# AdaLN attention and expert layer: a new order of work ahead of the first attention step

## The reference

```python
mod = (silu(c) @ wmod).reshape(1, 6, 1, 256)       # sa, ca, ga, sb, cb, gb
h = layernorm(x) * (1 + ca) + sa
q = (h @ Wq).reshape(1024, 16, 16); k = (h @ Wk).reshape(1024, 4, 16); v = (h @ Wv).reshape(1024, 4, 16)
q, k = rope(q), rope(k)                            # rotates the first 8 of the 16 numbers of a head
attn = softmax(q @ k.T * 16 ** -0.5)               # 4 query heads share a head of k and v
x = x + ga * (attn @ v) @ Wo
```

## Time and profile before

| what | us |
|---|---|
| median of 3 runs (528.10, 524.89, 522.38) | 524.89 |
| profiled execution, its own time | 527.01 |
| its span, first to last instruction | 525.2 |
| TensorE, VectorE, ScalarE, GpSimd busy | 467.3, 344.1, 217.1, 208.3 |
| mean granted clock of TensorE | 0.947 |

### The profile page before, as it was taken

How to read it: one execution, slowest core, us unless ns; L and a number is a source line. 1 busy time by engine, 2 the same in 40 slices (tenths; PEclk the granted TensorE clock), 3 DMA queues, 4 the chain that set the end, 5 groups by cost and what they waited for, 6 DMA issues and landing times.

```text
span 525.2 us, 7847 instructions
## 1 busy us (share of the span) xinstructions
PE 467.3 (89%) x2748; PEld 250.5 (48%) x2748; DVE 344.1 (66%) x751; ACT 217.1 (41%) x317; POOL 208.3 (40%) x209
## 2 busy tenths in 40 slices
PE   3958889999999999997896999899999998999890
PEld 3635222333333333223664767566666666666560
DVE  5597959999999999902276973655545454455247
ACT  1547437878878788794213231111111111111140
POOL 3366000212032021200312244567777777776503
PEclk9987769999999999999597999999999999999996
DMA  8970000000000000000101001068888888884181
GB/s 282 337 216 0 1 0 2 1 1 1 1 2 1 1 2 2 0 1 1 40 0 41 1 1 29 13 198 256 271 258 252 244 265 244 278 262 146 38 338 61
DMA packets 33617, 53.68 MB, mean 102 GB/s; under 512 B 6870, under 2 KB 21918, under 8 KB 33584
## 3 DMA queue, kind: packets, MB, share of 16 engines
q1 hardware_dynamic: 27728, 44.82, 26.8%
q0 software_dynamic: 5856, 8.43, 5.6%
HBM read 50.71 MB, written 10.09 MB: 116 GB/s over the span
## 4 chain that ended last, share of the span: by engine, by line
PE 58%; DVE 18%; DMA 9%; issue 6%; POOL 5%; ACT 4%; SPq 0%; DVEq 0%; POOLq 0%; ACTq 0%
PE PV L1221 12%; DMA ychoice<-QS,tab 8%; PE M L1175 7%; PE EP L1403 7%; PE EP L1208 5%; PE EP L1211 5%; PE EP L1299 4%; DVE mx L788 2%; POOL QS L449 2%; PE PV L1420 2%; DVE x L1056 2%; POOL ychoice L454 2%; PE M L1420 1%; DMA x<-in_x 1%; DVE QS L1008 1%
## 5 line engine op out<-in xcount | busy, mean ns | idle before, releaser
L788 DVE TENSOR_REDUCE mx<-M 128x1 f32<-128x512 f32 x256 | 159.3, 683 | 18.0 <-PE M L1175 17.8
L607 ACT ACTIVATE QS<-EP 128x1024 f32<-128x1024 f32 x128 | 123.9, 1021 | 24.9 <-PE EP L1211 24.6
L1403 PE MATMUL EP<-w,QS 128*128 128x352 f32 x244 | 85.2, 472 | 1.3 <-DVE QS L997 1.3
L659 ACT ACTIVATE QS<-EP 128x176 f32<-128x176 f32 x61 | 19.3, 317 | 138.7 <-PE EP L1403 138.7
L449 POOL DMA_INDIRECT QS<-h2rows,tab x61 | 63.1, 1035 | 31.0 <-issue 13.2
L454 POOL DMA_INDIRECT ychoice<-QS,tab x61 | 61.8, 1013 | 21.9 <-issue 15.9
L1221 PE MATMUL PV<-QS,VA 128*32 128x512 f32 x512 | 69.7, 617 | 0.0
L997 DVE COPY QS<-EP 128x256 f32<-128x256 f32 x61 | 25.7, 422 | 63.7 <-PE EP L1397 63.7
L1175 PE MATMUL M<-KT,QT 64*128 64x512 bf16 x256 | 61.9, 403 | 3.5 <-DVE mx L788 2.6
L1403 PEld LDWEIGHTS EP<-w,QS 128*128 128x128 f32 x244 | 43.4, 189 | 26.5 <-issue 11.0
L1208 PE MATMUL EP<-QT,KT 64*128 64x512 bf16 x256 | 49.6, 380 | 1.6 <-ACT QTB L564 1.2
(11 more groups left out here) (240 smaller groups left out, 640.9 us busy)
## 6 DMA issues: line engine op xcount, KB each, us to landing
w<-in_w SPq DMA_DIRECT2D x30, 704.0 KB
w<-in_w SPq DMA_DIRECT2D x61, 112.0 KB
w<-ychoice SPq DMA_DIRECT2D x8, 512.0 KB, 8.3
w<-in_w SPq DMA_DIRECT2D x30, 128.0 KB
segu<-in_segu SPq DMA_DIRECT2D x1, 1408.0 KB, 10.7
x<-in_x SPq DMA_DIRECT2D x2, 512.0 KB, 5.1
wide<-in_wmod SPq DMA_DIRECT2D x1, 1024.0 KB, 8.3
h2rows<-xh SPq DMA_DIRECT2D x2, 512.0 KB, 2.9
```

Source lines behind the costliest of these rows:

```text
L607: nc.scalar.activation(PT[n % 3][:, 2 * p:2 * p + 2, :], EP[p][:, :, :], ACT.Exp, scale=HD ** -0.5).then_inc(e_done, 1)
L788: nc.vector.tensor_reduce(out=mx[:, u % 2, s // 2, j, s % 2:s % 2 + 1], in_=src, axis=AX.X, op=ALU.max).then_inc(m_free, 1)
L1403: ins = mm(BANK[b][:, 0:I13], XGT[b][:, c * P:(c + 1) * P], w13[:, r, c * I13:(c + 1) * I13], start=c == 0, stop=c == NC - 1)
```

## The change

- The order of tiles: statistics and normalisation are done half by half, and TensorE transposes half 1 behind tile 3 instead of ahead of tile 2.
- TensorE begins with 14 matmuls of constants that nobody reads (`WARM`); the ten at the end of the pass (L1254) go.
- VectorE rotates and splits half 0 alone; GpSimd rotates half 1 and splits its K. Two memsets of `KSB` and one of `QSB` go from GpSimd to VectorE's start; GpSimd's copies of V to `VA` go behind `minus_max(0)`. `KSB`, `KTB` and the rotation's scratch move to other tensors.
- The pass runs through the four query tiles against keys 0 to 511 first, then against the others (`max_part`). It starts when two groups of half 0 are evacuated. A new `QK` of 16 groups, all by ScalarE, is spread by `QK_COUNT`: two groups in steps 0, 1, 5, 6, 7 and 8, one in steps 3 and 4.
- The later modulation rows and columns (`later_mod`) lie in the pass, behind steps 2, 5 and 6, one bank at a time.
- `transpose_B(0)` comes inside step 8, and scores of attention step 0 inside step 9.

```diff
-    Q_FILL, O_FILL = [4 * LEAD + 1], []
+    Q_FILL, O_FILL = [4 * NT + 3], []
...
+    WARM = 14
...
-        KSB = hT[:, :, :].rearrange("p c s -> p (c s)").bitcast(bf16).rearrange("p (t g c) -> p t g c", t=NT, g=NG)
+        KSB = QS[:, NT * NH * AR:].rearrange("p (t g c) -> p t g c", t=NT, g=NG)
...
-        rt = xh[:, :, :].rearrange("p t n -> p (t n)")[:, 0:16 * (NH + NG) * 4].rearrange("p (k t n) -> p k t n", k=4, t=4)
+        QTf = QT[:, :, :].rearrange("p h s -> p (h s)").bitcast(f32)
+        rt = [v[:, 0:16 * (NH + NG) * 4].rearrange("p (k t n) -> p k t n", k=4, t=4)
+              for v in (QTf, hT[:, :, :].rearrange("p c s -> p (c s)"))]
...
-        KTB = wide[:, NC * D:NC * D + NG * S // 2].bitcast(bf16).rearrange("p (g s) -> p g s", g=NG)
-        QTf = QT[:, :, :].rearrange("p h s -> p (h s)").bitcast(f32)
+        KTB = xh[:, :, :].rearrange("p t n -> p (t n)").bitcast(bf16).rearrange("p (g s) -> p g s", g=NG)
...
-        QK = [(0, "K", 0, 0), (0, "Q", 0, 0), (0, "K", 1, 0), (1, "K", 1, 0), (0, "Q", 0, 2), (0, "K", 0, 2),
-              (1, "K", 0, 2), (1, "Q", 0, 0), (0, "K", 1, 2), (1, "K", 1, 2), (1, "Q", 0, 2), (0, "Q", 0, 4),
-              (1, "Q", 0, 4), (0, "Q", 0, 6), (1, "Q", 0, 6)]
-        QK_DVE = (1, "K", 0, 0)
-        Q1_M, Q1_COPY = 3, 4
-        K_LAST = 1 + max(n for n, item in enumerate(QK) if item[1] == "K")
+        QK = [(0, "K", 0, 0), (0, "Q", 0, 0), (0, "Q", 0, 2), (0, "K", 0, 2), (0, "Q", 0, 4), (0, "Q", 0, 6),
+              (1, "K", 0, 0), (1, "K", 0, 2), (1, "Q", 0, 0), (1, "Q", 0, 2), (0, "K", 1, 0), (1, "K", 1, 0),
+              (1, "Q", 0, 4), (1, "Q", 0, 6), (0, "K", 1, 2), (1, "K", 1, 2)]
+
+        QK_COUNT, MOD_AT = (4, 6, 6, 7, 8, 10, 12, 14, 16, 16), (2, 5, 6)
+        K0_MAX, K1_MAX, Q1_MAX = 2, 7, 9
+
+        def max_part(k):
+
+            u, i = divmod(k, NT)
+            return u, i % 4, i // 4
...
+        def rope_parts(h):
+
+            tt = slice(4 * h, 4 * h + 4)
+            pr = qkv[:, tt, 0:(NH + NG) * HD].rearrange("p t (h i two) -> p t h i two", h=NH + NG, two=2)
+            cs = [w[:, tt, :].unsqueeze(2).to_broadcast([P, 4, NH + NG, 4]) for w in (cosr, sinr)]
+            R = [rt[h][:, k].rearrange("p t (h i) -> p t h i", i=4) for k in range(4)]
+            return pr[:, :, :, 0:4, 0], pr[:, :, :, 0:4, 1], cs, R
...
+            pool.wait_ge(s_ident, 2)
+            pool.tensor_copy(identb[:, :], ident[:, :]).then_inc(s_ident, 1)
+            pool.memset(VA[:, :, :, :], 0.0).then_inc(s_va, 1)
+            pool.wait_ge(s_va, 1)
+            pool.memset(VA[:, :, :, HD:HD + 1], 1.0).then_inc(s_va, 1)
...
-            pool.memset(QSB[:, :, :, BR:AR], 0.0).then_inc(s_pad, 1)
-            pool.wait_ge(s_ident, 2)
-            pool.tensor_copy(identb[:, :], ident[:, :]).then_inc(s_ident, 1)
...
-            for h in range(2):
-                tt = slice(4 * h, 4 * h + 4)
-                pool.wait_ge(s_qkvev, 4 * h + 4)
-                pool.tensor_copy(VA[:, tt, :, 0:HD],
-                                 qkv[:, tt, (NH + NG) * HD:].rearrange("p t (g d) -> p t g d", g=NG)).then_inc(s_va, 1)
-
-            for i in range(2):
-                pool.memset(KSB[:, :, :, AR * i + BM:AR * i + AR], 1.0).then_inc(s_pad, 1)
...
-                pool.wait_ge(s_ks, h + 1)
+                pool.wait_ge(s_ks, 1)
+                pool.wait_ge(s_k1, 5 * h)
...
-            parts_of_k_in_B(0)
+            pool.wait_ge(ld_rope, 32)
+            pool.wait_ge(s_qkvev, NT)
+            turned = [0]
+
+            def then(ins):
+                turned[0] += 1
+                ins.then_inc(s_turn, 1)
+                pool.wait_ge(s_turn, turned[0])
+
+            a, b, cs, R = rope_parts(1)
+            pool.tensor_tensor(R[0], a, cs[0], ALU.mult)
+            pool.tensor_tensor(R[1], b, cs[1], ALU.mult)
+            pool.tensor_tensor(R[2], a, cs[1], ALU.mult)
+            then(pool.tensor_tensor(R[3], b, cs[0], ALU.mult))
+            pool.tensor_tensor(a, R[0], R[1], ALU.subtract)
+            pool.tensor_tensor(b, R[2], R[3], ALU.add).then_inc(s_ropes, 1)
+            pool.wait_ge(s_ropes, 1)
+            pool.tensor_copy(k_parts(KSA, 1, 0, 1), residual(1, NH)).then_inc(s_k1, 1)
+            pool.wait_ge(s_k1, 1)
+            pool.tensor_tensor(residual(1, NH), residual(1, NH), k_parts(KSA, 1, 0, 1), ALU.subtract).then_inc(s_k1, 1)
+            pool.wait_ge(s_k1, 2)
+            pool.tensor_copy(k_parts(KSA, 1, 1, 1), residual(1, NH)).then_inc(s_k1, 1)
+            pool.wait_ge(s_k1, 3)
+            pool.tensor_copy(k_parts(KSA, 1, 2, 2), k_parts(KSA, 1, 0, 2)).then_inc(s_k1, 1)
+            pool.wait_ge(s_k1, 4)
+            pool.tensor_copy(k_parts(KSA, 1, 4, 4), k_parts(KSA, 1, 0, 4)).then_inc(s_k1, 1)
             pool.wait_ge(s_qs, 1)
             pool.tensor_tensor(q1, q1, q_part(1, 0), ALU.subtract).then_inc(s_qs, 1)
+            parts_of_k_in_B(0)
             parts_of_k_in_B(1)
             pool.wait_ge(s_split, 2)
             parts_of_q_in_B(0)
             pool.wait_ge(s_qs, 3)
             parts_of_q_in_B(1)
             minus_max(0)
+            for h in range(2):
+                tt = slice(4 * h, 4 * h + 4)
+                pool.tensor_copy(VA[:, tt, :, 0:HD],
+                                 qkv[:, tt, (NH + NG) * HD:].rearrange("p t (g d) -> p t g d", g=NG)).then_inc(s_va, 1)
...
             for t in range(NT):
-                if t == 2:
+                if t == 4:
                     rows_T1(2)
                     rows_T1(3)
+                if t == 6:
+                    act.wait_ge(s_split, 1)
+                    q_copy(0, 1, 0)
+                if t == 7:
+                    act.wait_ge(s_split, 2)
+                    q_copy(0, 3, 2).then_inc(s_qa, 1)
                 act.wait_ge(s_qkv, t + 1)
                 nc.scalar.activation(qkv[:, t, :], BANK[(7 + t) % 8][:, 0:QKV], ACT.Copy).then_inc(s_qkvev, 1)
...
-            act.wait_ge(s_split, 1)
-            q_copy(0, 1, 0)
-            act.wait_ge(s_split, 2)
-            q_copy(0, 3, 2).then_inc(s_qa, 1)
-            act.wait_ge(s_rope, 2)
+            def qk(n):
+
+                act.wait_ge(s_qk, n + 1)
+                dst, src = qk_evac(QK[n], BANK[n % 4])
+                nc.scalar.activation(dst, src, ACT.Copy).then_inc(s_qkA, 1)
+
+            def later_mod(b):
+
+                act.wait_ge(s_mod, b + 2)
+                if b < 2:
+                    ins = nc.scalar.activation(MOD[:, 2 + 2 * b:4 + 2 * b, :], BANK[6].rearrange("p (b n) -> p b n", b=2), ACT.Copy)
+                else:
+                    ins = nc.scalar.activation(modc[:, 3:5, :], BANK[6][:, 2 * NC:4 * NC].rearrange("p (k c) -> p k c", k=2), ACT.Copy)
+                ins.then_inc(s_modev, 1)
+
+            for n in range(6):
+                qk(n)
+            act.wait_ge(s_ropes, 1)
             nc.scalar.activation(q_part(1, 0), q1, ACT.Copy).then_inc(s_qs, 1)
-            act.wait_ge(s_mod, 2)
-            for b in range(2):
-                nc.scalar.activation(MOD[:, 2 + 2 * b:4 + 2 * b, :], BANK[4 + b].rearrange("p (b n) -> p b n", b=2), ACT.Copy).then_inc(s_modev, 1)
-            nc.scalar.activation(modc[:, 3:5, :], BANK[3][:, 2 * NC:4 * NC].rearrange("p (k c) -> p k c", k=2), ACT.Copy).then_inc(s_modev, 1)
-            for n, item in enumerate(QK):
-                if n == Q1_M:
-                    act.wait_ge(s_qs, 2)
-                    q_copy(1, 1, 0)
-                    nc.scalar.activation(q_part(1, 2), q1, ACT.Copy).then_inc(s_qs, 1)
-                if n == Q1_COPY:
-                    act.wait_ge(s_qs, 3)
-                    q_copy(1, 3, 2).then_inc(s_qa, 1)
-                act.wait_ge(s_qk, n + 1)
-                dst, src = qk_evac(item, BANK[n % 4])
-                nc.scalar.activation(dst, src, ACT.Copy).then_inc(s_qkA, 1)
+            act.wait_ge(s_qs, 1)
+            q_copy(1, 1, 0)
+            later_mod(0)
+            qk(6)
+            qk(7)
+            act.wait_ge(s_qs, 2)
+            nc.scalar.activation(q_part(1, 2), q1, ACT.Copy).then_inc(s_qs, 1)
+            act.wait_ge(s_qs, 3)
+            q_copy(1, 3, 2).then_inc(s_qa, 1)
+            for n in range(8, len(QK)):
+                qk(n)
+                if n == 10:
+                    later_mod(1)
+                if n == 12:
+                    later_mod(2)
...
+            nc.vector.memset(QSB[:, :, :, BR:AR], 0.0).then_inc(s_pad, 1)
+            for i in range(2):
+                nc.vector.memset(KSB[:, :, :, AR * i + BM:AR * i + AR], 1.0).then_inc(s_pad, 1)
...
             for h in range(2):
                 dve.wait_ge(ld_x[h], 16)
                 statistics(h, s_var)
-            for h in range(2):
                 dve.wait_ge(s_rstd, h + 1)
                 normalise(h, s_h)
                 if h == 0:
...
-            dve.wait_ge(s_tr, NT // 2)
-            for h in range(2):
-                tt = slice(4 * h, 4 * h + 4)
-                dve.wait_ge(s_qkvev, 4 * h + 4)
...
-            dve.wait_ge(s_qkd, 1)
```

(106 more changed lines are left out.)

56 lines of the change are left out of this document (9 added, 47 removed).

## The result

The changed kernel takes 519.49 us (median of 5 runs, 518.06 to 519.74), the kernel before 524.20 (5 runs, 522.38 to 528.10). The ratio is 0.988, with a 95% interval of 0.984 to 0.992: 6.2 us gained, between 4.1 and 8.3, where 11.0 were forecast. The profiled execution took 519.49 with a span of 517.7. Its mark of the loop, the scores of the third step, stands at 74.03 us against 80.45 before, 6.4 us earlier, and the last copy of attention's output at 248.55 against 255.15, 6.6 earlier. So the gain is made by the third step and is carried on one for one.

A forecast was written before the change was run, and what follows sets the result against it. A chain of waits to the first scores at 74.17 us, then a TensorE-bound loop. First scores at 62.75, 11.4 us earlier, less 0.4 for the pair, gave 11.0 gained: 513.9 us beside the median 524.89, range 505 to 520.

The forecast's parts named there:

- the course I gave 0.50 to: Main forecast for the whole kernel: 11.0 us gained, 513.9 us, within 511 to 517, chance 0.50.
- its own signs: Wrong if granted clock in the pass is 0.5 for over 4 us, QKV starts at full clock, or loop's step changes.
- The rotation on GpSimd: Second half's rows: six operations near 31 us, mean near 0.75 us, 4.5 us in all, rotated at 35.4.
- the low level of the first transposes: Transposes ahead of QKV stay at 1.2 GHz, near 0.43 us each, against 0.27 at high clock.
- the loop's step of 2.5: Attention loop is TensorE's, some 2.5 us a step, unchanged; its end moves one for one with its start.
- Three memsets: VectorE's start: memsets taken over from GpSimd, together 5.9 us at GpSimd's price, from about 0.8 to 6.8.
- The warm-up: Fourteen 512-column matmuls before the weights land: no direct cost, low clock again at the transposes, no gain.
- GpSimd late: Rival: GpSimd at twice the price or worse, VectorE waits for second-half K and Q; 519 to 523 us, chance 0.08.
- The walk of the queues: Pass: VectorE dry 0.3, 0.7, 1.5 and 2.2 us at steps 4 to 7; 32nd maximum ends at 57.4.
- clock low in part of the pass: Rival: lean steps 3 and 4 drop the clock, steps 5 and 6 take some 7 us; 517 to 521, chance 0.14.
- First scores behind their maximum: End of the pass: from the 32nd maximum at 57.4 to first scores at 62.75, against 74.17 before.
- The dip of the clock at 76.5 to 79: Loop's start: two steps at 6.1 us instead of 5.0, left as it was.

The follow-up runs named there:

- e1: Changed kernel without its 14 warm-up matmuls (WARM = 0); 518.71 us, ratio 0.989 to the kernel before.
- e2: Changed kernel with the modulation in steps 2, 3 and 4 instead of 2, 5 and 6; 514.77 us, ratio 0.981 to the kernel before.
- e6: Changed kernel with rotation and K's split of the second half back on VectorE instead of GpSimd; 522.53 us, ratio 0.995 to the kernel before.
- e3: Changed kernel plus five unread 512-column matmuls behind each of steps 3 and 4; 516.39 us, ratio 0.983 to the kernel before.
- e5: Changed kernel with ScalarE's two Q copies of the second half ahead of its evacuation of group 7; 514.37 us, ratio 0.982 to the kernel before.
- e4: Changed kernel plus five unread 512-column matmuls behind step 8, ahead of the loop; 516.88 us, ratio 0.986 to the kernel before.
- e9: e8 with transposes moved ahead, up to three groups a step, none left for steps 8 and 9; 509.87 us, ratio 0.971 to the kernel before.
- e10: e9 with modulation columns and first filler exchanged (columns in step 4, filler in step 3); 508.80 us, ratio 0.971 to the kernel before.
- e12: e10 with five filler matmuls ahead of B's transposes and three behind step 8; 509.01 us, ratio 0.969 to the kernel before.
- e11: e10 with the five filler matmuls behind step 8 moved ahead of B's transposes; 508.20 us, ratio 0.967 to the kernel before.
- e8: Changed kernel with modulation rows ahead of pass and in step 2, columns in step 3, filler behind steps 4 and 8, Q copies first; 511.43 us, ratio 0.977.
- e7: Changed kernel with the later modulation in one piece ahead of the pass, as before; 518.45 us, ratio 0.989 to the kernel before.

## Why the prediction was right in sign and too large

**Luck in the number.** The range of 505 to 520 holds the measured 519.49 by half a microsecond, and not by the course I gave 0.50 to: forecast were 513.9 us and a gain of 11.0, measured 6.2. By its own signs the prediction is wrong: the granted clock was at 0.50 in the pass from 43.3 to 50.2 us, where over 4 us were to mean that; the first scores came at 64.8, not at 62 to 63, and VectorE was dry for 7.6 us, not some 4. The rotation on GpSimd, the low level of the first transposes and the loop's step of 2.5 came as written. An earlier start (2.6 us, not foreseen) hid over a third of what was lost later.

**Up to the pass: 2.6 us better than forecast.** Three memsets took 3.5 us together, not 5.9: I had taken GpSimd's price, with bounds of 1.9 and 6.3 from VectorE's own rows. (In proportion to the rows named there the bounds are 2.5 and 7.0.) The Trainium skill's rule that was weighed ("VectorE: DVE Perf Modes", "Zero memsets can be issued as uint32 (trn2)") came out too slow for both shapes: the zeros did go out as 1920 uint32, and that took 1.66 us where one element a cycle makes 2.0 by the clock of that page's table, and the 1024 bf16 of ones took 0.91 where it makes 1.07. The same section says that a zero memset of bf16 can go out as uint32, half as many elements. I left that out of the estimate of 6.1; with it the page's figures make an estimated 4.1 us. With the memsets done early the transposes start at 10.69 instead of 12.7. The rest is 0.4 us less for QKV, which I don't account for. VectorE's rotation and split took 6.9 us, forecast 7.1, which makes up the rest.

**The warm-up** at nothing: right in time as far as e1 can tell, and in the level of the first transposes and of the first QKV tile. The level was up before them (1.92 us for the columns in e2) and fell at 9 to 12 us; in the changed kernel it fell at 9.2, while the columns ran, so the idle stretch that I gave as the reason isn't all of it.

**GpSimd:** six operations at a mean of 0.77, forecast 0.74; K's parts done at 36.2, forecast 38.7, and TensorE transposes them in step 3, at 38.79, without a wait. The rival "GpSimd late" is out, and e6 shows what its part is worth.

**The pass: 7.6 us dry instead of 4.7.** The walk of the queues had 0.3, 0.7, 1.5 and 2.2 us at steps 4, 5, 6 and 7, at 2.4 GHz. Measured are 0.92 ahead of step 3 (behind the modulation rows of step 2, which the walk had as hidden), 1.64 within step 5, 3.14 ahead of step 6 and 1.94 ahead of step 7. The third and largest is four matmuls of rows that take 3.35 us instead of 1.98. My rival "clock low in part of the pass" had this, with the lean steps 3 and 4 as its cause, at 517 to 521 and a chance of 0.14; it is the case that came. e3 speaks for the mechanism: with filler in just those steps the level held through 54 us. The clock isn't all of the miss: with the level high, the waits ahead of steps 6 and 7 are still 1.36 and 1.94 us in e3.

**First scores behind their maximum:** 5.35 us forecast from the last maximum to the scores, 6.85 measured (57.93 to 64.78); the groups of transposes took 1.03 to 1.06 instead of 0.62. In e5, with the level high there, negated maximum to scores took 5.2 (56.17 to 61.35).

**The step that failed** is the sentence "The dip of the clock at 76.5 to 79, where two steps took 6.1 us instead of 5.0, I leave as it was", and with it the same assumption for all of the new stretch. I treated the dip as belonging to the place. The runs tie it to what TensorE did before: without filler ahead of the loop the two steps took 8.1 to 9.3 us in seven profiles of seven, with it 6.1 in six of six. The sentence also misread its rows: the two steps took 6.28, and as they take 6.07 with the clock at 1.00 throughout (e4), the dip's share was about 0.2 us and not 1.1. What I carried over was nearly the price at the high level. In the changed kernel they took 9.25 us; my sum had 6.7, the 6.3 of before and 0.4 for the pair that now follows the scores: 2.6 us too little. The three differences, 0.5 at the 32nd maximum, 1.5 from there to the scores and 2.6 in the first steps, are the 4.6 us by which the third step missed its forecast of 69.45 (62.75 and 6.7). e4 closes the largest of them: 3.3 us in the trace from five matmuls in an idle wait.

I counted the ten unread matmuls as 4.5 us of removed work and never asked what else they did. The Trainium skill has the rule beside it, "TensorE: Matmul & The Clock Gate", "Part 4: PE-mode transpose": by it, transposes don't count as busy for the clock in the same way as matmuls. I dismissed it on one stretch at 1.00 with three groups a step. The traces give the rule a part: with one group a step and nothing else the level fell at 42 to 43 us, in the changed kernel and in e1, e4 and e5, and with three groups a step it held in e9, e10 and e12 but fell once in e11 (0.82 from 40 to 48). I had costed a leaner mixture by the denser one's row, and the denser one isn't safe either. What made the level fall the second time, at 57 us, no run isolates. A rival stands: the sixteen one-column matmuls of the modulation. Of the twelve kernels that have them inside the pass, the level fell while they ran or soon after them in eight (the changed kernel, e1, e2, e3, e4, e6, e8 and e11), and held well beyond them in four (e5, e9, e10 and e12). No kernel leaves only them out of the pass.

**What stays open.** The trace of the changed kernel has 6.4 to 7.5 us of gain, the ratio 6.2 with 4.1 to 8.3, so nothing is left over there. Why the clock holds in one execution and falls in another in the same gap of 1.67 us ahead of the pass isn't settled: it held in the changed kernel, e1, e4 and e5 and fell in e2 and e3. With modulation rows in that gap it held in all five (e8 to e12). The same holds within the pass, for e8's fall at 42 and e11's at 45. The spread shows in the times too: of e7's eight executions the three with a mean granted clock of 0.951 took 516.6 to 516.9 us, the five with 0.941 to 0.945 took 518.4 to 520.6. How large the gains of e2 to e5 over the changed kernel are isn't settled either: the intervals of their ratios overlap with its own, and only those of e8 to e12 are clearly below it. That there is a gain is likely: all sixteen executions of the four (513.67 to 517.25) lie below all five of the changed kernel (518.06 to 519.74), though they weren't timed beside one another.

## What to carry to other kernels

When a change thins out or reorders TensorE's work ahead of a TensorE-bound loop, price the new stretch at both clock levels, and ask of each piece of "useless" work that it removes whether it kept the level up for what follows. A filler is cheap where TensorE waits anyway: five matmuls in a 2 us wait gave 3.3 us in the trace; but price it at the low level too. Once the level has fallen it takes nearly twice as long, which in e4 still fitted the wait and in e10 held up what follows by 1.7 us; put ahead of the fall (e11) it took 1.25 or less. A profile is one execution, and the level differs between executions of one program, so look at several before a fall is put down to an edit. Work moved into a pass that another engine bounds isn't hidden there unless each step has room for it: here the same modulation in one piece ahead of the pass cost no more.

## What the runs showed of the hardware

- A zero memset of 3840 bf16 on VectorE was executed as 1920 uint32 in 1.66 us, 3.39 on GpSimd; one of 1024 bf16 ones took 0.91 on VectorE, against 1.26 on GpSimd.
- With GpSimd's memset gone from beside it, the second normalisation took 1.38 us instead of 4.99.
- Sixteen one-column matmuls, TensorE busy throughout (7.32 to 10.9 in e1), didn't raise the clock: the transposes behind them took 1.09 us for four, where 0.60 is the high level's time (19.23 in e1). Behind fourteen matmuls of 512 columns the same sixteen took 1.92 us instead of 3.54 (e2).
- The level outlived idle stretches of 1.14 and 0.99 us ahead of the loop in e8, 0.88 in e11, 1.11 ahead of 46.77 in e3 and 1.67 ahead of the pass in the changed kernel; it fell in the same 1.67 us in e2 and e3 and behind a wait of 1.14 us in e10. What counts is more than the gap itself.
- From 7 to 16 us the stage view's granted clock read 1.00 in e1 while transposes took 1.09 us for four, as they did in the changed kernel, where it read 0.50 from 10 to 16; durations are the better witness there.
